# Attention in shifted windows: the softmax shift made on TensorE from the maximum itself, instead of from a product that GpSimd makes

## The reference

```python
xn = _layernorm(xt, norm1_g, norm1_b)                       # then rolled by 3 and cut in windows of 49 tokens
qkv = (xw @ qkv_w + qkv_b).reshape(Bw, N, 3, HEADS, dh).transpose(2, 0, 3, 1, 4)
q, k, v = (qkv[0], qkv[1], qkv[2])
attn = jnp.einsum('bhnd,bhmd->bhnm', q, k) * dh ** (-0.5)
attn = jax.nn.softmax(attn + bias, axis=-1)
out = jnp.einsum('bhnm,bhmd->bhnd', attn, v).transpose(0, 2, 1, 3).reshape(Bw, N, C)
out = out @ proj_w + proj_b
```

## Time and profile before

| | |
|---|---|
| runs shown | 1978.91, 1980.95, 1982.73 us |
| median | 1980.95 us |
| span of the profiled execution | 1974.3 us |
| PE busy | 1764.7 us, 89% of the span |
| PEld busy | 1091.3 us, 55% |
| DVE busy | 1361.2 us, 69% |
| ACT busy | 1540.4 us, 78% |
| POOL busy | 1171.4 us, 59% |
| mean granted TensorE clock | 0.956 |

### The profile page before, as it was taken

The page is one execution under the profiler, slowest core; times in us unless marked ns, Lnnn a source line. Parts: engine busy times, 40 slices in busy tenths (PEclk is TensorE's granted clock), DMA queues, the critical chain, the costliest instruction groups (busy, mean ns, idle before and its releaser), DMA issues. The chain is left out here.

```text
span 1974.3 us, 90330 instructions
## 1 busy us (share of the span) xinstructions
PE 1764.7 (89%) x38186; PEld 1091.3 (55%) x38186; DVE 1361.2 (69%) x2016; ACT 1540.4 (78%) x2904; POOL 1171.4 (59%) x1048
## 2 busy tenths in 40 slices
PE   4999999999999999999999999985999958999994
PEld 2666656565666556565666656541699943333331
DVE  7776767676776667676776767543777757888872
ACT  3788888888888888888888888865666639988880
POOL 5677777777787777878787777742355530221222
PEclk9999999999999999999999999995899975999998
DMA  3343554444443444344444444322478758999983
GB/s 111 101 100 101 143 130 112 101 115 99 110 105 102 102 102 114 99 113 103 108 107 102 106 102 105 77 55 65 133 216 216 216 117 171 264 260 244 248 226 110
DMA packets 233227, 262.26 MB, mean 133 GB/s; under 512 B 167078, under 2 KB 179910, under 8 KB 232710
## 3 DMA queue, kind: packets, MB, share of 16 engines
q1 hardware_dynamic: 217478, 217.50, 45.0%
q0 software_dynamic: 15360, 39.08, 6.6%
HBM read 160.82 MB, written 80.88 MB: 122 GB/s over the span
## 5 line engine op out<-in xcount | busy, mean ns | idle before, releaser
L416 POOL TENSOR_TENSOR shift<-const_b,qmax 113x588 bf16<-113x588 bf16 x256 | 299.3, 1169 | 224.8 <-DVE qmax L511 223.2
L563 DVE TENSOR_TENSOR x<-ps_m,x 112x392 f32<-112x392 f32 x128 | 66.5, 562 | 267.0 <-PE ps_m L1028 267.0
L511 DVE TENSOR_REDUCE qmax<-ps_s 113x12 f32<-113x588 f32 x256 | 194.7, 761 | 65.2 <-PE ps_s L907 65.1
L1481 POOL DMA_DIRECT2D out_rolled<-r_OUT x128 | 63.8, 503 | 284.5 <-DVE r_OUT L1581 284.5
L716 ACT ACTIVATE P<-ps_t 113x588 f32<-113x588 f32 x256 | 171.9, 672 | 52.9 <-PE ps_t L959 52.2
L748 ACT ACTIVATE G<-ps_m 128x392 f32<-128x392 f32 x384 | 178.1, 499 | 43.1 <-PE ps_m L1009 43.0
L503 DVE TENSOR_TENSOR Ul<-Uf 113x784 bf16<-113x784 f32 x192 | 206.1, 1100 | 0.0
L1333 PE MATMUL conv_ps<-xin,band_now 64*64 64x448 bf16 x2688 | 202.7, 364 | 2.2 <-DVE x_low L1228 2.2
L406 POOL TENSOR_TENSOR xhl<-xh 113x784 bf16<-113x784 f32 x64 | 202.3, 3161 | 2.2 <-DVE xh L551 2.2
L709 ACT COPY Uf<-ps_m 113x392 f32<-113x392 f32 x384 | 172.6, 485 | 31.4 <-PE ps_m L874 23.2
L1333 PE MATMUL conv_ps<-x_low,band_now 64*64 64x448 bf16 x1344 | 176.5, 351 | 0.0
(11 more groups left out here) (239 smaller groups left out, 5201.1 us busy)
## 6 DMA issues: line engine op xcount, KB each, us to landing
xin<-rows_scratch SPq DMA_DIRECT2D x96, 236.0 KB, 3.7
XT<-x_tokens SPq DMA_DIRECT2D x64, 294.0 KB, 3.2
X<-x_windows SPq DMA_DIRECT2D x128, 147.0 KB, 3.3
RS<-rs_scratch SPq DMA_DIRECT2D x128, 147.0 KB, 3.3
XR<-x_windows SPq DMA_DIRECT2D x128, 147.0 KB, 3.2
x_scratch<-x SPq DMA_DIRECT2D x128, 147.0 KB, 3.4
y_scratch<-y POOLq DMA_DIRECT2D x96, 196.0 KB, 2.8
r_RS<-rs_scratch SPq DMA_DIRECT2D x128, 147.0 KB, 4.7
```

The source lines that it names most:

```text
L416: nc.gpsimd.tensor_tensor(shift[:, j % 2], e, m, ALU.mult).then_inc(S["md"], 1)
L511: nc.vector.tensor_reduce(qmax[:, j % 2, :].rearrange("p (b n) -> p b n", b=2), ps_s[0:R, :, 0:2 * HQ].rearrange("p b (n t) -> p b n t", t ...
```

## The change

The shift is made by PE from the maximum itself. The stationary operand is now one column of `qmax`, repeated 49 times by a stride of zero, and the moving operand is the negative identity: out[key, query] is the sum over partitions p of max[p] times -1 where p is the query. Since each window and head has a column of its own, it takes 24 matmuls of 49 columns for a quad in place of four of 294. The maximum is written as bfloat16, as the product was. The step `make_shift`, its buffer, its semaphore `md` and the block of ones go. PE waits for `mx` where it waited for `md`, and DVE's maximum waits for `st` of two quads before where it waited for `md`.

```diff
-        qmax = sb("qmax", [R, 2, QP * HEADS])
-        shift = sb("shift", [R, 2, QP * HEADS, TOK], BF16)
+        qmax = sb("qmax", [R, 2, QP * HEADS], BF16)
...
-            def make_shift(s, j):
-
-                if s.real:
-                    q = 4 * s.n + j
-                    wait(pool, S["mx"], q + 1)
-                    wait(pool, S["st"], q - 1)
-                    m = qmax[:, j % 2, :].unsqueeze(2).to_broadcast([R, QP * HEADS, TOK])
-                    e = minus_eye.unsqueeze(1).to_broadcast([R, QP * HEADS, TOK])
-                    nc.gpsimd.tensor_tensor(shift[:, j % 2], e, m, ALU.mult).then_inc(S["md"], 1)
...
             def step(s):
-                old, prv, nxt, nx2 = s.at(-2), s.at(-1), s.at(1), s.at(2)
-                make_shift(s, 1)
+                old, prv, nx2 = s.at(-2), s.at(-1), s.at(2)
                 wrap_columns(s.at(-3))
-                make_shift(s, 2)
-                make_shift(s, 3)
                 x1_low(prv)
                 low1(old)
                 centre_tokens(s.at(4))
-                make_shift(nxt, 0)
                 squares_low(prv)
                 low0(nx2)
...
                     wait(dve, S["s_q"], q + 1)
-                    wait(dve, S["md"], q - 1)
+                    wait(dve, S["st"], q - 1)
                     nc.vector.tensor_reduce(
...
                     q = 4 * s.n + j
-                    wait(pe, S["md"], q + 1)
+                    wait(pe, S["mx"], q + 1)
                     for b in range(2):
                         if b == 1:
                             wait(pe, S["kb"], q + 1)
-                        m = shift[:, j % 2, 2 * HEADS * b:2 * HEADS * (b + 1), :].rearrange("p (n h) t -> p n (h t)", n=2)
-                        for g in range(2):
-                            lo = ROWB * g
-                            ins = mm(onto_scores(b, g), group_ones[lo:lo + TOK, lo:lo + TOK], m[lo:lo + TOK],
-                                     start=False, stop=True)
+                        for k in range(2):
+                            for h in range(HEADS):
+                                n, at = HEADS * (2 * b + k) + h, SV * k + TOK * h
+                                for g in range(2):
+                                    lo = ROWB * g
+                                    ins = mm(ps_t[lo:lo + TOK, b, at:at + TOK],
+                                             qmax[lo:lo + TOK, j % 2, n:n + 1].to_broadcast([TOK, TOK]), minus_eye[lo:lo + TOK],
+                                             start=False, stop=(k == 1 and h == HEADS - 1))
                     ins.then_inc(S["st"], 1)
```

More of the change, by code:

```diff
@@ L56 @@
 PACK_A, WIDE_A = columns(
-    ("center", R), ("picks", 2 * R + TOK), ("eye_c", 2 * (C + 1)), ("last_row", C + 1), ("key_ones", 4 * DH),
+    ("center", R), ("picks", R + TOK), ("eye_c", 2 * (C + 1)), ("last_row", C + 1), ("key_ones", 4 * DH),
     ("qkv_w", 3 * C), ("fc1_w", HID), ("w2_own", ROWB), ("sums", 2 * R), ("eps0", 1), ("rows", 3 * C + HID), ("norms", 4),
@@ L137, in attention_phase @@
         const_f = packed("picks", R)
-        const_b = sb("const_b", [R, 2 * R + TOK], BF16)
+        const_b = sb("const_b", [R, R + TOK], BF16)
         pick = const_b[:, 0:R]
-        group_ones = const_b[:, R:2 * R]
-        minus_eye = const_b[:, 2 * R:2 * R + TOK]
+        minus_eye = const_b[:, R:R + TOK]
         key_ones = packed("key_ones", R).rearrange("p (a d) -> p a d", a=2)
@@ L243, in attention_phase @@
         margins_stored = sem("margins_stored")
-        names = ("t_sum t_mean t_cen t_sqr t_var t_ln t_rs xh0 lo0 uu u_hi u_lo s_q mx kb md st ex vev pv lnd rdn nrm "
+        names = ("t_sum t_mean t_cen t_sqr t_var t_ln t_rs xh0 lo0 uu u_hi u_lo s_q mx kb st ex vev pv lnd rdn nrm "
                  "proj x1_made x1_lo cen xc sq sq_lo var ln rs xh1 lo1 f1 ge f2 x2_made").split()
@@ L1772, in constants @@
     out["last_row"] = np.eye(1, C + 1, C, dtype=f)
-    pick, ones, minus = np.zeros((R, R), f), np.zeros((R, R), f), np.zeros((R, TOK), f)
+    pick, minus = np.zeros((R, R), f), np.zeros((R, TOK), f)
     for j in range(TOK):
@@ L1780, in constants @@
         lo = ROWB * g
-        ones[lo:lo + TOK, lo:lo + TOK] = 1
         for b in range(2):
             key_ones[lo:lo + TOK, b, DH * (g ^ b):DH * (g ^ b) + DH] = 1
-    out["picks"] = np.concatenate([pick, ones, minus], 1)
+    out["picks"] = np.concatenate([pick, minus], 1)
     out["key_ones"] = key_ones.reshape(R, 4 * DH)
```

## The result

| | before | changed |
|---|---|---|
| runs | 1977.88 to 1982.73 us (4) | 2066.67, 2066.77, 2074.37, 2087.14 us |
| median | 1979.93 us | 2070.57 us |
| ratio | | 1.0449, 95% interval 1.0415 to 1.0483 |
| profiled execution | span 1974.3 us | 2087.14 us, span 2085.5 us |
| POOL busy | 1171.4 us | 834.4 us |

The change makes the kernel 4.5% slower, 91 us, where 9 were forecast. The profiled execution is the slowest of the four, some 20 us above the fastest, so what is read from it is the upper side.

What follows compares the result with a forecast made beforehand. PE was taken to bound most of a strip, with ACT and DVE leading in places. 64 strips x 0.14 = 9.0, less 0.1, is +8.9 us; 1974.3 + 8.9 + 6.7 = 1989.9 us, range 1979 to 2000.

Steps and rivals of the forecast that it cites:

- Matmul rounds, 0.07 us more a quad: Shift on PE: 12 rounds of 49 columns take 0.32 us where two of 294 took 0.25.
- On the path for quads 0 and 1, covered for 2 and 3: PE's longer shift counts in full for quads 0 and 1, 0.14 us a strip; waits hide the others.
- GpSimd's product worth nothing: Removing GpSimd's multiply, 299 us busy beside PE, gives nothing by itself, as no PE wait names it.
- the waits worth nothing: PE's wait for DVE's maximum is empty; DVE's wait for the shift, up to 0.17 us, is taken as nothing.
- The side term: DVE's token mean, 0.49 us as a rule, 0.17 at least, loses the multiply beside it, offsetting the later maximum.
- A: Rival: no change, the shift's rounds run at column time, 0.245 us, or a wait covers them; 1980 us, chance 0.18.
- C: Rival: faster, DVE sets the pace up to fc1 and a strip gains some 0.15 us; 1971 us, chance 0.12.
- B: Rival: shift's weight loads not hidden, each waiting for the matmul before it in its quadrant; 2049 us, chance 0.10.
- its mark, groups of 0.8 us: Sign in the trace for unhidden weight loads: the shift's matmul groups on PE would span 0.8 us.
- The sum: Over 64 strips of the attention phase, 0.14 us each is 9.0, less 0.1 at the start: +8.9 us.
- the forecast term: PE's longer shift rounds on the path for quads 0 and 1, forecast at 0.14 us a strip over 64 strips.
- Around the span: Outside the profiled span: 6.7 us between the span and the runs' median, taken not to change.

Runs made afterwards that it cites:

- e3: Changed kernel with four matmuls of 294 columns from a fixed tile of zeros in place of the 24, shift not computed: 1981.19 us, 0.9998 of the kernel before.
- e5: Changed kernel with four buffers for DVE's maximum in place of two: 2065.79 us, ratio 1.0390 to the kernel before.
- e1: Kernel before, GpSimd's product kept, only the shift's four matmuls of 294 columns cut into 24 of 49: 2050.28 us, ratio 1.0342.
- e9: Kernel before with the bias left out of the query scores, four matmuls of 294 columns fewer a quad: 1993.03 us, ratio 1.0051.
- e7: Changed kernel with half of the query scores' matmuls left out: 1997.93 us, ratio 1.0078 to the kernel before.
- e4: Changed kernel with thin loads beside attention, 8 columns in place of 784 or 672: 2019.36 us, ratio 1.0202 to the kernel before.
- e8: Kernel before with thin loads beside attention, 8 columns in place of 784 or 672: 1975.30 us, ratio 0.9959.

## Why the prediction was wrong

The sign was right and the time was far outside the range. By its steps:

- **Matmul rounds, 0.07 us more a quad:** right. The group spans 0.47 us against 0.48 worked out; in the trace its rounds of two matmuls start 0.026 us apart. So the round over two quadrants costs what the one over four did. The Trainium skill has a floor of about 25 ns from one matmul to the next ("TensorE: Matmul & The Clock Gate", Back-to-back issue gap). Read for the matmuls of one quadrant, it agrees within 1 ns; the two of a round, in different quadrants, start 1 ns apart or less.
- **On the path for quads 0 and 1, covered for 2 and 3:** right. An undisturbed strip grew by 0.11 us, forecast 0.14. This term is some 7 us of the 91.
- **GpSimd's product worth nothing, the waits worth nothing:** right for a PE with its old count, shown by e3 (0.9998). With the stops DVE does wait for the shift, 42 us; whether that reaches the end stays open (e5). The side term too: the token mean, 0.49 us beside the product, is 0.175 in the middle of its records now, and PE did not wait for it.
- **Rivals:** A and C did not come. B, the load that is not hidden, would have given 2049, close to the total of e1 by accident: its mark, groups of 0.8 us, is absent, and the loads stay hidden beside matmuls of the same rows. The Trainium skill's rule that a weight load overlaps matmuls only in other rows (the same page, The mechanism) is against the trace here as it was before.
- **The step that failed:** the sum took for PE only the time that the array needs. The 20 extra loads and 20 extra matmuls a quad were counted as rounds and never as instructions that must be brought in. The sentence was "so the work is in rounds of two matmuls"; a term for the supply was left out, that is put at nothing without a reason. What the runs put in its place: PE's instructions come in blocks of 256. Fetches started no closer than 3.5 us to one another in the change (3.3 in any run), three in four of them 4.1 or more, also where PE needed them sooner. Before, a strip took 996 instructions in 20.1 us, a block in 5.2. The change adds 160 and makes it 4.5, if nothing stops, and dense places such as 24 scores and 24 shifts in a row go through their part of a block much faster. The sum had nothing for it; in the profiled execution the stops alone are 43 us, and up to 82 with the lower clock.
- **What the loss is made of, an estimate for the profiled execution** (112 us longer in this phase): 47 - 4 = 43 us of stops; 85 - 7 = 78 us more at the lower clock, at most half of it lost, 39; the forecast term 7; 10 of waits at fc1 behind DVE (L996 and `xc`), which e1 has too; 11 less of gelu. That makes 88; the other 24 are not assigned to a row.
- **Around the span:** the sum put 6.7 us between a span and its run's time. The runs whose time and span are both known show 1.6 to 1.7, so the profiled execution before was some 5 us faster than the median. The forecast does not move by it, since its 8.9 us were set upon the median all the same.

A sign of it stood in the trace of before and was not used. The waits of the kernel before over its attention phase hold this line, and the order in time holds one such stop:

```profile
PE ps_s L907 <- issue: 2.4, 4, 0.9
```

```profile
649.68 0.26 PE L907 MATMUL ps_s<-xh,Uf 49*49 49x49 bf16 x10 [0.79 <-issue]
```

A stop of 0.79 us after 14 of 24 matmuls that wait for nothing, and at a seam, says that in places the supply was already at its edge.

Open: why the change costs some 20 us more than e1 with as many instructions; how much of the lower clock is due to the stops, since e9 and e7 show it with few (e7: 44 us at the lower level, none of its 10 stretches close behind a stop); and what holds a fetch back after a seam, beside the data on the DMA engines. One more difference was seen and not tested: 31 of DVE's 192 casts to `Ul` take over 2 us, where 3 did before and 18 do in e1.

## What to carry to other kernels

Before small matmuls take the place of few long ones in straight-line code, divide PE's instructions, loads included, by the time they run in, and compare with the pace of the instruction queue; an equal column count is no equal cost. In the profile, look for "issue" waits in the middle of a run of equal instructions, and count the instructions between them. GpSimd was off the path here, so taking its work away by giving more to PE had only a price (e3: 0.9998 without the extra matmuls).

## What was not expected of the hardware

- PE's instructions arrive in 16 KB blocks of 256: the packets of the page's instruction queue grew by 40 for 10240 more matmuls and loads. A block that is not there stops PE for up to 2.9 us at a seam, and all 74 stops of the change stand at seams. PE goes on 1.2 to 1.6 us after the missing packet's end.
- Only the next block is fetched ahead: its packet starts 0.5 to 3.0 us after PE has passed a seam (nine in ten of the change), and no closer than 3.3 us to the packet before it in any run.
- Other DMA traffic makes it worse: with the DMA share down from 0.40 to 0.21 the same instructions cost 2.4% in place of 4.5% (e4 over e8).
- The clock often falls around a stop: where it did at the one that ended at 673.01, the four projection matmuls took 2.95 us in place of 1.57. But it falls without stops as well (e9, e7).
- Less work for PE can be slower: e9 took four matmuls a quad out, the mean granted clock of the profiled execution fell from 0.956 to 0.941, and the time rose by 0.5% (0.25 to 0.76).
